# The first attention of a two-layer hybrid, rebuilt on the plan of the second: scores twice, a turned exponential, both batches of a head group in a row

## The reference

```python
x = x + attn_a(layernorm(x))      # latent attention with rotation
x = x + ffn(layernorm(x))         # 8 experts, 2 of them per token
x = x + attn_b(layernorm(x))      # plain attention
x = x + ffn(layernorm(x))

# attn_a: x is [16, 256, 128], 16 heads of 8, latent width 32
q, k, v = split(x @ c_attn_w.T + c_attn_b)               # per head: 8 wide
q_lat, k_lat, v_lat = q @ q2l_w.T + q2l_b, k @ kv2l_w.T + kv2l_b, v @ kv2l_w.T + kv2l_b
q_lat = q_lat * cos + rotate_half(q_lat) * sin           # pairs (even, odd) of the 32
k_lat = k_lat * cos + rotate_half(k_lat) * sin
att = softmax(causal((q_lat @ wqk_w.T + wqk_b) @ k_lat.T * 32 ** -0.5))
y = (att @ v_lat) @ l2o_w.T + l2o_b, then all heads @ cproj_w.T + cproj_b
```

## Time and profile before

| | us |
|---|---|
| median of three executions | 1537.97 |
| lowest and highest of them | 1536.82, 1553.16 |
| the profiled execution | 1552.42 |
| its span, first to last instruction | 1550.6 |
| mean granted TensorE clock in it | 0.841 of full speed |

### The profile page before, as it was taken

How to read it: one execution, slowest core, us unless ns; L and a number is a source line. 1 busy time by engine, 2 the same in 40 slices (tenths; PEclk the granted TensorE clock), 3 DMA queues, 4 the chain that set the end, 5 groups by cost and what they waited for, 6 DMA issues and landing times.

```text
span 1550.6 us, 31022 instructions
## 1 busy us (share of the span) xinstructions
PE 1256.5 (81%) x10131; PEld 993.8 (64%) x10132; DVE 875.0 (56%) x2055; ACT 730.0 (47%) x2046; POOL 679.7 (44%) x896
## 2 busy tenths in 40 slices
PE   3799999999999999656999378888899855899700
PEld 2577777777777777546999245555666534899600
DVE  3535666656655765585554156666655638455322
ACT  0145666546655657303554345576656520455300
POOL 0303132213212230057552666777756516755276
PEclk9759999879989999857999577899878855899855
DMA  8000000000000000002223000000000000233232
GB/s 204 1 1 1 2 8 2 10 1 8 1 9 1 8 1 8 27 1 57 76 76 58 24 18 15 21 22 22 12 11 8 8 27 0 72 75 77 52 80 73
DMA packets 56253, 45.75 MB, mean 30 GB/s; under 512 B 13570, under 2 KB 48258, under 8 KB 56130
## 3 DMA queue, kind: packets, MB, share of 16 engines
q0 software_dynamic: 9088, 18.63, 5.7%
q1 hardware_dynamic: 39378, 22.44, 5.1%
q10 hardware_dynamic: 7664, 3.04, 0.9%
HBM read 27.57 MB, written 16.52 MB: 28 GB/s over the span
## 4 chain that ended last, share of the span: by engine, by line
PE 50%; issue 17%; POOL 13%; DVE 11%; ACT 4%; DMA 3%; ACTq 1%; DVEq 0%; POOLq 0%
PE PS L1759 9%; PE PS L1423 7%; PE PS L1425 5%; PE PS L1424 5%; POOL got L649 5%; PE PS L1505 3%; PE PS L1674 3%; PE PS L1487 2%; PE PS L1724 2%; DVE X L1195 2%; DMA b_cols<-in_L_ffn_b_dram 2%; POOL rope_q L579 2%; PE PS L1491 2%; PE PS L1621 2%; PE PS L1525 1%
## 5 line engine op out<-in xcount | busy, mean ns | idle before, releaser
L1222 ACT ACTIVATE prob<-PS,neg_max 128x128 f32<-128x128 f32 (+1 forms) x512 | 210.1, 422 | 203.2 <-DVE neg_max L890 202.6
L890 DVE TENSOR_REDUCE neg_max<-PS 128x2 f32<-128x512 f32 (+1 forms) x192 | 131.6, 688 | 119.7 <-PE PS L1491 117.7
L688 POOL DMA_INDIRECT xg<-normed,source x156 | 151.6, 972 | 100.8 <-PE PS L1737 69.2
L1349 ACT ACTIVATE hid<-PS,b_cols 128x256 f32<-128x256 f32 x312 | 122.6, 476 | 86.2 <-PE PS L1425 86.2
L649 POOL DMA_INDIRECT got<-expert_rows,slot_of x128 | 122.2, 954 | 80.5 <-DMA expert_rows<-y_rows 46.2
L1759 PE MATMUL PS<-W,hid 128*128 x1248 | 152.4, 275 | 1.9 <-ACT hid L1349 1.8
L1303 ACT ACTIVATE PT<-PS 128x768 f32<-128x768 f32 x128 | 103.6, 810 | 97.2 <-PE PS L1652 96.1
L1759 PEld LDWEIGHTS PS<-W,hid 128*128 128x128 f32 x1248 | 146.2, 192 | 2.6 <-issue 2.6
L612 POOL TENSOR_SCALAR_AFFINE_SELECT PT<-PT 128x256 f32<-128x256 f32 x256 | 99.0, 411 | 105.1 <-ACT PT L1303 104.7
L1505 PE MATMUL PS<-C,prob 128*128 128x128 f32 x768 | 125.7, 290 | 5.4 <-issue 5.3
L579 POOL TENSOR_TENSOR rope_q<-rope_q 128x512 f32<-128x512 f32 x32 | 41.3, 1290 | 196.5 <-DVE rope_q L869 196.5
(11 more groups left out here) (280 smaller groups left out, 3237.9 us busy)
## 6 DMA issues: line engine op xcount, KB each, us to landing
expert_rows<-y_rows SPq DMA_DIRECT2D x78, 128.0 KB, 1.8
normed<-xn SPq DMA_DIRECT2D x16, 256.0 KB, 2.3
xg<-normed,source POOLq DMA_INDIRECT x156, 2.7
W<-in_L_ffn_w_dram SPq DMA_DIRECT2D x1, 2048.0 KB, 15.8
got<-expert_rows,slot_of POOLq DMA_INDIRECT x128, 2.5
out_dram<-X SPq DMA_DIRECT2D x8, 256.0 KB, 2.4
b_rows<-in_L_ffn_b_dram SPq DMA_DIRECT2D x2, 512.0 KB, 3.6
X<-in_L_attn_a_x_dram ACTq DMA_DIRECT2D x2, 256.0 KB, 4.4
```

The costliest lines, as they stand in the source:

```text
L688: nc.gpsimd.indirect_dma_start(out=xg[:, i % 4, b_, :], out_offset=None, in_=normed, in_offset=bass.IndirectOffsetOnAxis(ap=source[:, k:k ...
L890: v.tensor_reduce(neg_max[:, nb, 0:heads], s_bank[nb][:, :].rearrange("p (h k) -> p h k", h=heads), AX, ALU.max, negate=True).then_inc(m[" ...
L1222: ins = s.activation(prob[:, nb, cols], s_bank[nb][:, cols], ACT.Exp, bias=neg_max[:, nb, h:h + 1], accum_out=sums[:, u // G, min(nb, 1), ...
L1349: ins = s.activation(hid[:, r % 2, k, :], h_bank[r % 2][k // 2][:, k % 2 * ROWS:(k % 2 + 1) * ROWS], ACT.Gelu, bias=b1_cols[:, bass.ds(e * ...
```

## The change

The first attention becomes a plan like the second's (`PlanA`), written out with no loop. Steps per unit: an early one (query or key projection for two pairs of units ahead), a late one, and in even units an extra one. A unit is one batch of one head group, and the two batches of a group follow each other, so a pair of units shares a query, a key and a latent query. Tiles for these are rings of three.

- Query and key: one projection each. ScalarE adds the bias (`whole`), GpSimd multiplies with the cosine (`start_rope`), VectorE swaps neighbouring partitions and multiplies with a signed sine (`swap`), GpSimd adds (`end_rope`).
- The latent query comes as the late step of an even unit; ScalarE writes it whole and its high half, VectorE the low half (`query_low`). ScalarE makes the key's high half, GpSimd the low one.
- Scores: three half products, each in two groups of four matmuls. Turned scores: the same three in two groups of two, and then the turned maxima, which ScalarE copied out (`max_t`), through a selection matrix.
- Exponential, triangle, value product and turn as in the second attention; `cproj` is taken in the order of pairs of groups. The sums come from columns of ones, written once in the preparation, so GpSimd no longer resets `v_aug` after the first attention.
- Normalisation moves from VectorE to ScalarE. The first attention's output bias is added by GpSimd ahead.
- The opening makes groups 0 and 1 only, and two split matrices instead of four.
- The helpers of both attentions are merged; in the second attention no instruction changes its place.

The diff, cut to what the order of work needs:

```diff
+class PlanA:
+    FIRST = [("prep", 0, 7), ("query", 0, 6), ("key", 0, 5), ("value", 0, 4), ("query", 1, 7), ("key", 1, 6), ("query2", 0, 5)]
+    LATE = [None, ("turn", 1, -1), None, ("prep", 0, 1), None, ("value", 0, 1), None, ("gate_t", 0, -1)]
+    EXTRA = [("gate", 0, -2), None, ("out_t", 0, -1), None, ("out", 0, -1), None, ("turn", 0, 0), None]
...
 GpSimd
-                    nc.gpsimd.tensor_tensor(rope_q[:, 0, :], rope_q[:, 0, :], rope_q[:, 1, :], ALU.add).then_inc(m["summed"], 1)
+                for unit in range(NCH * UNITS):
+                    if u % 2 == 0 and unit // 2 + 1 < NCH * G:
+                        key_low(unit // 2 + 1)
+                    if early:
+                        start_rope(early)
+                    mask(m, unit, 0)
+                    if early:
+                        end_rope(early)
+                    mask(m, unit, 1)
+                    if unit + 1 < NCH * UNITS and normal_a(unit + 1):
+                        root(m, normal_a(unit + 1)[1])
...
 VectorE
+                def swap(s):
+                    own.then(v.stream_shuffle(swapped[:, which, :], whole[:, which, :], [l + 1 - 2 * (l % 2) for l in range(L)]))
+                    v.tensor_tensor(pair, pair, con("sin").unsqueeze(1).broadcast_to([P, 2, S]),
+                                    ALU.mult).then_inc(m["keys_swapped" if which else "queries_swapped"], 1)
...
+                for unit in range(NCH * UNITS):
+                    if unit + 1 < NCH * UNITS:
+                        row_max(m, unit + 1, 0)
+                    if plan.late[unit]:
+                        closing(m, w, plan.late[unit], True)
+                    if u % 2 == 0 and unit // 2 + 1 < NCH * G:
+                        query_low(unit // 2 + 1)
+                    if plan.early[unit]:
+                        swap(plan.early[unit])
+                    if plan.extra[unit]:
+                        closing(m, w, plan.extra[unit], True)
...
 ScalarE
+                for unit in range(NCH * UNITS):
+                    copy_max(unit)
+                    if plan.early[unit]:
+                        step(plan.early[unit])
+                    if u % 2 == 0 and unit // 2 + 1 < NCH * G:
+                        key_high(unit // 2 + 1)
+                    exponent(m, unit, 0)
+                    if unit and unit % G == 0:
+                        copy_o(m, unit // G - 1)
+                    if plan.late[unit]:
+                        step(plan.late[unit])
+                    exponent(m, unit, 1)
+                    if plan.extra[unit]:
+                        step(plan.extra[unit])
+                    if normal_a(unit):
+                        normal("a", *normal_a(unit), c - 1)
...
 TensorE
+                    for last, (q, k) in enumerate(((q_h, k_h), (q_l, k_h), (q_h, k_l))):
+                        for j in range(G):
+                            t_.matmul(bank[j][:, 0:P], q[rows, i3, b_, 0:P], k[rows, i3, b_, 0:P], start=False, stop=False, skip_group_check=True)
+                        for j in range(G):
+                            ins = t_.matmul(bank[j][:, P:3 * P], q[rows, i3, b_, P:S], k[rows, i3, b_, :], start=False, stop=(last == 2), skip_group_check=True)
...
+                    pe.wait_ge(m["mt_copied"], unit + 1)
+                    for h in range(2):
+                        t_.matmul(bank[4 + h][:, 0:S], sel_r[rows, :], max_t[rows, :, :].rearrange("p b q -> p (b q)"), start=False, stop=False, skip_group_check=True)
...
+                for unit in range(end):
+                    turn_max(m, unit)
+                    if unit + 1 < end:
+                        causal((2, 3))
+                    if plan.early[unit]:
+                        step(plan.early[unit])
+                    if unit + 1 < end:
+                        pe.wait_ge(m["mt_copied"], unit + 1)
+                        causal((0, 1))
+                        scores(unit + 1)
+                    turned_scores(unit, 0)
+                    if unit:
+                        value_product(unit - 1)
+                    if plan.late[unit]:
+                        step(plan.late[unit])
+                    turned_scores(unit, 1)
+                    if plan.extra[unit]:
+                        step(plan.extra[unit])
```

More of the change, by code:

```diff
@@ L191, in __init__, with number @@
         self.kind, self.g, self.c, self.bank = kind, g, c, bank
-        self.by_act = kind in ("query", "key", "out_t", "gate_t")
+        self.by_act = kind in ("query", "key", "query2", "out_t", "gate_t")
+def number(steps):
+    last, freed, kinds = {}, {True: 0, False: 0}, {}
+    for k, s in enumerate(steps):
+        s.made = k + 1
+        freed[s.by_act] += 1
+        s.freed = freed[s.by_act]
+        s.before = last.get(s.bank)
+        last[s.bank] = s
+        kinds[s.kind] = kinds.get(s.kind, 0) + 1
+        s.stacked = kinds[s.kind]
+    return {(s.kind, s.g, s.c): s for s in steps}
@@ new lines, with __init__, find @@
+class PlanA:
+    FIRST = [("prep", 0, 7), ("query", 0, 6), ("key", 0, 5), ("value", 0, 4), ("query", 1, 7), ("key", 1, 6), ("query2", 0, 5)]
+    LATE = [None, ("turn", 1, -1), None, ("prep", 0, 1), None, ("value", 0, 1), None, ("gate_t", 0, -1)]
+    EXTRA = [("gate", 0, -2), None, ("out_t", 0, -1), None, ("out", 0, -1), None, ("turn", 0, 0), None]
+    LAST = [("gate", 0, -1), ("turn", 1, 0), ("out_t", 0, 0), ("out", 0, 0), ("gate_t", 0, 0), ("gate", 0, 0)]
+    def __init__(self):
+        self.prologue = [Step(k, g, 0, bank) for k, g, bank in self.FIRST]
+        self.early, self.late, self.extra = [], [], []
+        for unit in range(NCH * UNITS):
+            c, u = divmod(unit, UNITS)
+            ahead, g = divmod(unit // 2 + 2, G)
+            self.early.append(Step("key" if u % 2 else "query", g, ahead, 7) if ahead < NCH else None)
+            near, g = divmod(unit // 2 + 1, G)
+            if u % 2:
+                kind, g, dc = self.LATE[u]
+                self.late.append(Step(kind, g, c + dc, 7) if 0 <= c + dc < NCH else None)
+                self.extra.append(None)
+            else:
+                self.late.append(Step("query2", g, near, 7) if near < NCH else None)
+                kind, g, dc = self.EXTRA[u]
+                self.extra.append(Step(kind, g, c + dc, 7) if 0 <= c + dc else None)
+        self.epilogue = [Step(k, g, NCH - 1 + dc, 7) for k, g, dc in self.LAST]
+        in_cycles = itertools.chain(*zip(self.early, self.late, self.extra))
+        self.steps = [*self.prologue, *(s for s in in_cycles if s), *self.epilogue]
+        self.at = number(self.steps)
+    def find(self, kind, g, c):
+        return self.at[kind, g, c]
@@ L195, with statistics_a, normal_a @@
+def statistics_a(unit):
+    c, u = divmod(unit, UNITS)
+    if u == 1 and c + 1 < NCH:
+        return c + 1
+    return c - 1 if u == 5 and c else None
+def normal_a(unit):
+    c, u = divmod(unit, UNITS)
+    if u == 2 and c + 1 < NCH:
+        return c + 1, norm_no(c + 1)
+    return (c - 1, gate_norm_no(c - 1)) if u == 6 and c else None
 class Plan:
@@ new lines, in causal, with turn_max @@
+            def causal(banks):
+                for j in banks:
+                    diagonal = bank[j].rearrange("p (a k) -> p a k", k=P)[:, 0:3:2, :]
+                    t_.matmul(diagonal, ident_b[:, :], causal_b[:, :].unsqueeze(1).broadcast_to([P, 2, P]), start=True, stop=False,
+                              skip_group_check=True)
+            def turn_max(m, unit):
+                pe.wait_ge(m["max_ready"], unit + 1)
+                for q in range(2):
+                    ins = t_.transpose(bank[q][:, 3 * P:4 * P], M[:, q, :], ident)
+                ins.then_inc(m["mt_ready"], 1)
@@ new lines, in weighted @@
+            def weighted(m, unit, g, b_, at):
+                pe.wait_ge(m["masked"], 2 * unit + 2)
+                if unit % G == 0 and unit:
+                    pe.wait_ge(m["o_copied"], unit // G)
+                for kb in range(2):
+                    for j in range(G):
+                        ins = t_.matmul(bank[6][j * L:(j + 1) * L, at + kb * P:at + S], v_aug[:, unit // UNITS % 2, 2 * b_ + kb, g * G + j, :],
+                                        PT[:, unit % 2, j, kb * S:kb * P + S], start=(unit % G == 0 and kb == 0), stop=(g % 2 == 1 and kb == 1),
+                                        skip_group_check=True)
+                ins.then_inc(m["pv_ready"], 1)
@@ L1615, in step @@
[L1615 to L1622 removed]
+                    bank_free(m, s)
+                    common(m, w, plan, s, norm_b(s.c) if s.kind == "prep" else gate_norm_b(s.c), (0, 2, 1, 3))
```

993 lines of the change are left out of this document (365 added, 628 removed).

## The result

The changed kernel is 3.1% faster: ratio of its runs to those of the kernel before 0.9689, 95% interval 0.9587 to 0.9791. Its median is 1494.88 us over four runs (1485.49 to 1503.34), that of the kernel before, run beside it, 1545.57. The profiled execution took 1496.32 us, its span is 1492.7. Further down, the profiled executions of norm_late and changed_again are among the slower of their kernels, so of these two only pairs at full clock are read, and of the second the half clock as a measure of scatter.

What follows compares the result with a forecast made beforehand. TensorE was taken to bound the first attention, and a chain over ScalarE and VectorE its new form: 496 us at full clock, 534 with half clock, plus 979 outside the 64 units, gave 1513 us; range 1460 to 1568.

Steps and rivals of the forecast that it cites:

- the case called likeliest: Whole kernel: 1493 to 1529 us, with a share of 0.10 to 0.28 of the stage at half clock; chance 0.37.
- The opening: Before the first attention's units: first transposes at 42.4 us, unit 0 at 65.5, 20.7 us earlier than before.
- The chain of the even unit: First attention: latent query, ScalarE's copies, VectorE's low half, swap and sine product end 9.05 us in, then the extra step's emptying.
- The second pair: Second pair of units in a chunk: 15.3 us, ScalarE's normalisation and a transpose copy standing ahead of the copy of maxima.
- the stall of 1.0 from a collision: Fourth pair of a chunk: 1.0 us added for VectorE's low half waiting on GpSimd where a root comes late.
- a sign of being wrong: New profile, first attention: pairs of units under 14.5 us or over 17 would count against the forecast.
- expected sine products of over 2 us: First attention, VectorE: sine products would at times take over 2 us, held up by GpSimd through their two SBUF inputs.
- TensorE waiting for masks: New profile, first attention: this wait, instead of about 2 us for VectorE's emptying of bank 7, would count against the forecast.
- A share of 0.20 at half clock: First attention's 64 units: granted clock 0.90, so 496 us at full clock becomes 534.
- Waits are covered: Rival: extra step and swap overlap better, pairs take 14.2 to 15.2 us, kernel 1433 to 1476 us; chance 0.20.
- Slower, by the clock: Rival: TensorE's idle of 2 us once a pair drops it to half clock, kernel over 1% slower; chance 0.23.
- The step that rested on the earlier trace: Kernel before, first attention: a half-clock stretch begins right after TensorE idled 2.46 us at the loop's jump back.

Runs made afterwards that it cites:

- norm_late: The changed kernel with ScalarE's normalisation at the end of units 2 and 6 moved behind the next unit's copy of turned maxima; ratio to the kernel before 0.969.
- changed_again: The changed kernel run again without any edit; ratio to the kernel before 0.953, median 1500.35 us.
- fill: The changed kernel with TensorE writing the same causal masks again (4, 1, 6, 10 matmul pairs) in its idle before odd units' projections; ratio to the kernel before 0.935.
- swap_first: The changed kernel with VectorE's partition swap and sine product put ahead of the query's low half in even units; ratio to the kernel before 0.936.
- sine_twice_odd: The changed kernel with VectorE's sine product run twice in odd units, once into a spare tile; ratio to the kernel before 0.980.
- project_twice: The changed kernel with each query and key projection of the first attention made twice into the same bank; ratio to the kernel before 0.962.
- sine_twice_even: The changed kernel with VectorE's sine product run twice in even units, once into a spare tile; ratio to the kernel before 1.018.
- before_unrolled: The kernel before with only the loop over pairs of chunks of its first attention written out; ratio to the kernel before 0.994.
- fill_others: The changed kernel with repeated causal masks in the first three pairs' idle (4, 1, 6 matmul pairs), none in the fourth; ratio to the kernel before 0.955.
- fill_fourth: The changed kernel with repeated causal masks only in the longest idle, 10 matmul pairs in a chunk's last unit; ratio to the kernel before 0.961.

## Why the prediction was right, and where it was not

1513 was forecast, and the profiled execution took 1496.3, the median 1494.9. The forecast of faster by over 1% holds, and the time lies at the lower edge of the case called likeliest (1493 to 1529). The gain is larger than forecast, 3.1% by the ratio where 1513 lay 1.6% under the median. By its steps:

**The opening held.** First transposes at 42.66 (42.4 forecast), unit 0 at 65.03 (65.5). The working has a slip of 0.85 us: its listed terms add up to 18.65, not 19.5. By them unit 0 would begin 22.35 us behind the first transposes; it began 22.37 us behind.

**The chain of the even unit held.** In the third pair the projection starts 10.01 us behind the start of the unit; 9.05 + 0.75 was forecast. The latent query starts at 4.74, forecast 4.34. The pair took 16.24, forecast 16.1. The swap took 0.72 us, forecast 0.69. The Trainium skill, VectorE: DVE Perf Modes, The perf-mode tier table, had given 0.60 by estimate; the measured 0.72 decides. Six groups of scores took 0.79 us (302.07 to 302.86), not 0.99: 0.13 a group in the mean.

**Two terms were too large.** The second pair took 14.3, not 15.3: ScalarE's normalisation does hold the copy of maxima up (norm_late), but by 0.6 to 1.0 us. The fourth took 15.24 (in fill; the changed kernel has none at full clock), not 16.45: the stall of 1.0 from a collision did not come. The first took 14.21, not 14.85: its projection starts at 8.88 instead of 9.30 and the rest takes 5.33 instead of 5.55. With that two of the four pairs lie under 14.5 us, which the prediction had named as a sign of being wrong. In the 64 units the low half takes 0.76 us in the mean and the sine product 0.72:

```profile
L875 DVE TENSOR_TENSOR swapped<-swapped,C 128x512 f32<-128x512 f32 x60 | 43.0, 717 | 2.1
L881 DVE TENSOR_TENSOR q_l<-q_w,q_h 128x512 fp32r<-128x512 f32 x31 | 23.6, 760 | 78.9 <-ACT q_h L1157 78.9
```

That is from the groups by form of VectorE's lines, 65 to 585 us. The expected sine products of over 2 us are not there (the longest in the 64 units takes 1.14), and the reason stands in the timeline above: GpSimd has idled 2.58 us when it starts its last rotation step, because it waits for this very product. The order of the work keeps the two apart. With the order changed they collide (swap_first), by 0.45 to 0.65 us in each of the four rows shown. The rule of the Trainium skill, SBUF — State Buffer, Who interferes with whom, that a VectorE instruction with two SBUF inputs and a GpSimd one that reads SBUF exclude each other, agrees with these rows; where one engine waits for the other, it has nothing to exclude. The prediction had priced the rule without asking whether both engines are at work at that moment.

**A chain was left out.** "TensorE waiting for masks" was named as a sign that the prediction is wrong. It does so, 0.52 us in the third pair, and sine_twice_odd shows that a chain over VectorE's product of the odd unit ends in this wait, in three pairs of four. It stands ahead of the latent query, from which the first chain is counted, so it adds to that: the 0.52 us, less 0.20 that the score groups took less, are most of the 0.4 by which the latent query starts late. But a projection more in each unit of a pair costs 0.5 to 1.0 us and not 1.4 (project_twice), so TensorE's removed projections were worth less than their length.

**The clock was worse than forecast, and the chain better.** At full clock the 64 units are worth 524.1 - 0.4 x 135 = 470 us by estimate (135 us of half clock up to the last value product), where 496 was forecast: 8 x 2.7 = 22 us in the chunks' pairs, the rest in the last units. A share of 0.20 at half clock was forecast, and it is 0.26, and each us of it cost 0.4 instead of 0.35: 54 us, where 38 was forecast. The 17 us between forecast and result are 26 of a shorter chain, 8 of the stretch behind and 0.5 of the opening, less 16 of clock and 2 around the span. The sum came out close partly by luck: two terms missed in opposite directions.

**The rivals.** "Waits are covered" would have been 1433 to 1476. In the changed kernel the waits are not covered; fill and swap_first reach that range. "Slower, by the clock" was a real danger: sine_twice_even, with 0.69 us more a pair, is this rival come true (1578 us; the rival's figure was 1580). Its argument against, that half clock closes the gap that caused it, holds only in part: behind the 2.38 us the clock came back after 3 to 17 us, in time for the next idle. The step that rested on the earlier trace rows, that 2.46 us of idle at the loop's jump brought on the half clock there, is refuted for its case by before_unrolled: without that idle it begins at the same time. In the new stage filling the idles does take the half clock away (fill).

**What stays open.** Why half clock begins at 300.4 us in the kernel before, with or without the idle. Why idles of one length are followed by half clock in most cases in fill_others (six of seven), in fewer in sine_twice_odd (two of six), and why project_twice, with its long idles left in place, has half as much of it. No run here shows what decides that.

## What to carry to other kernels

Count the closed chain over all engines for each half of a period, not only from the longest visible wait; the test is to double one instruction in one place and in the other, and to read the length of a period at full clock, which repeats to 0.05 us where totals scatter by 1%. Where TensorE idles a microsecond or two in each period, the clock can cost more than the idle: here 0.7 us more chain a pair cost 12 us by itself and 71 by the clock. Repeating a matmul whose result stays the same in such an idle was free here and gave the clock back; taking work off another engine's chain gave both.

## What the runs showed of the hardware

- Adding work made the kernel faster: 21 pairs of bf16 matmuls a chunk gave a ratio of 0.935 where the changed kernel had 0.969 and 0.953, and with the projections made twice it was no slower.
- Full clock lasted 433 us in a row where TensorE idled 0.84 us at most up to the last unit (fill), and half clock began behind idles of 1.10, 1.55 and 2.38 us in kernels that had them, though not behind each: five of twelve idles of 1.10 and 1.55 in fill_fourth, six of seven of 2.2 to 2.4 in fill_others, two of six of 2.38 in sine_twice_odd. It also began behind idles of 0.54 and 0.84 us (fill_fourth, 352.6 us), and in before_unrolled three times with TensorE busy for 20 us ahead but for 0.21 us at most.
- One us at half clock cost 0.39 to 0.42 us in this stage. ScalarE and VectorE keep their pace in it: in the changed kernel a copy of 128 x 512 with bias took 0.687 us and a partition swap 0.72 us at either level.
- A partition swap of 128 x 512 fp32 on VectorE takes 0.715 to 0.748 us, a little more than an addition with two SBUF inputs of that size (0.69).
